# Attention with a SwiGLU block: group 0's rows of q and k replicated by TensorE, rotated rows of later batches copied by DMA, identity matmuls in TensorE's waits

## Time and profile of the kernel before

| | us |
|---|---|
| median of 3 runs (763.62 to 767.3) | 763.67 |
| the profiled execution, its own time | 764.55 |
| its span, first to last instruction | 762.6 |
| TensorE busy in the span | 718.3 |
| VectorE busy | 687.4 |
| ScalarE busy | 621.3 |
| GpSimd busy | 224.0 |
| first max unit starts at | 33.12 |
| first score matmul starts at | 67.94 |

### The profile page before, as it was taken

The page is one execution under the profiler, slowest core; times in us unless marked ns, Lnnn a source line. Parts: engine busy times, 40 slices in busy tenths (PEclk is TensorE's granted clock), DMA queues, the critical chain, the costliest instruction groups (busy, mean ns, idle before and its releaser), DMA issues.

```text
span 762.6 us, 13600 instructions
## 1 busy us (share of the span) xinstructions
PE 718.3 (94%) x4856; PEld 210.2 (28%) x4856; DVE 687.4 (90%) x1286; ACT 621.3 (81%) x1274; POOL 224.0 (29%) x364
## 2 busy tenths in 40 slices
PE   3798999999999999999999999999999999999987
PEld 1322223222222223232322223232322222232322
DVE  7788999999999999999999999999999999999931
ACT  1635888889898888989888888989888888989886
POOL 3756562216521563202121221202121121102100
PEclk9889999999999999999999999999999999999999
DMA  7511123011311103111110101111110101110021
...
DMA packets 29450, 34.35 MB, mean 45 GB/s; under 512 B 5672, under 2 KB 20264, under 8 KB 29256
## 3 DMA queue, kind: packets, MB, share of 16 engines
...
...
## 4 chain that ended last, share of the span: by engine, by line
PE 74%; DVE 16%; ACT 6%; DMA 2%; issue 2%; SPq 1%; ACTq 0%; DVEq 0%
PE acc_ps L1063 28%; PE banks L964 19%; DVE mx L810 13%; PE banks L984 10%; PE banks L988 6%; ACT probs L634 5%; PE banks L1070 4%; PE banks L1078 3%; PE banks L934 1%; PE banks L940 1%; PE banks L1113 1%; DMA k_rows<-part 1%; DMA y_all<-in_x 1%; PE banks L1086 1%; DMA qa<-q_rows 0%
## 5 line engine op out<-in xcount | busy, mean ns | idle before, releaser
L810 DVE TENSOR_REDUCE mx<-banks 128x1 f32<-128x512 f32 x1024 | 639.0, 684 | 34.5 <-PE banks L964 31.3
L634 ACT ACTIVATE probs<-banks 128x512 f32<-128x512 f32 x1024 | 549.2, 606 | 95.3 <-PE banks L984 90.3
L984 PE MATMUL banks<-qc,kc 51*128 51x512 bf16 x1024 | 304.6, 383 | 11.2 <-ACT probs L634 6.1
L964 PE MATMUL banks<-ka,qa 48*128 48x512 bf16 x1024 | 302.6, 384 | 7.2 <-DVE mx L810 6.6
L1063 PE MATMUL acc_ps<-probs,v_grp 128*32 128x512 f32 x2048 | 273.6, 606 | 1.2 <-ACT probs L634 1.0
L964 PEld LDWEIGHTS banks<-ka,qa 48*128 48x128 bf16 x1024 | 67.3, 94 | 293.9 <-DVE mx L810 249.9
L506 POOL TENSOR_TENSOR neg_max<-row_max,nought 128x16 bf16<-128x16 f32 x31 | 6.9, 222 | 317.5 <-DVE row_max L816 307.1
L984 PEld LDWEIGHTS banks<-qc,kc 51*128 51x128 bf16 x1024 | 64.6, 94 | 45.5 <-ACT probs L634 42.4
L988 PE MATMUL banks<-xn_T,w_ffn 128*128 128x256 f32 x192 | 65.8, 428 | 1.6 <-DVE w_ffn L804 1.6
L1063 PEld LDWEIGHTS acc_ps<-probs,v_grp 128*32 128x32 f32 x2048 | 40.3, 108 | 85.8 <-ACT probs L634 59.2
L529 POOL TENSOR_TENSOR gated<-gu 128x256 f32<-128x256 f32 x48 | 35.2, 734 | 73.9 <-ACT gu L695 73.9
...
## 6 DMA issues: line engine op xcount, KB each, us to landing
...
```

The lines of the kernel that those rows point to most:

```text
L634: nc.scalar.activation(probs[:, s % SLOTS, j, :], banks[:, score_bank(g, G * s + j), :], ACT.Exp, scale=SCALE).then_inc(exp_done, 1)
L810: nc.vector.tensor_reduce(out=mx[:, h, col, k:k + 1], in_=ps, op=ALU.max, axis=AX.X).then_inc(max_done, 1)
L964: nc.tensor.matmul(ps, qa[par][rows, j // 2, t * P:(t + 1) * P], ka[par][rows, k * W:(k + 1) * W], start=True, stop=True).then_inc(a_ready, 1)
L984: nc.tensor.matmul(banks[:, score_bank(g, u), :], kc[par][rows, kt * P:(kt + 1) * P], qc[par][rows, h, j // 2, :], start=True, stop=True). ...
```

## The change

- Group 0's stacked rows are no longer stored to HBM and loaded back. TensorE makes them: a matrix of ones and zeros (`select`, loaded by DMA) picks the rows of each part, 9 matmuls for each half of the positions, summed over the three parts in six PSUM banks; ScalarE copies the six banks into `ka[0]` and `qa[0]`, and six DMAs copy these into `kc[0]` and `qc[0]`. VectorE works half by half, and its root of batch 1 and its moments of batches 2 and 3 come between or behind; root of batches 2 and 3 comes behind the first reduction of a maximum.
- The rows of q and k are in the order dimension by head. The rotated rows of what is projected later are copies of the plain ones, made by four DMAs in SBUF for each batch (`load_twins`), and no longer projected.
- The last q rows of batch 0 and the k rows of batches 1 to 3 are summed in one bank from four full matmuls for each half, with weights that are zero outside a batch's rows.
- The transposition of batch 1, the projection of its q and the first feed-forward products move into the loop of the 48 max units; ScalarE now normalises batch 2, GpSimd batches 1 and 3.
- wf is loaded in two DMAs. TensorE multiplies the identity by itself 20 times ahead of its first wait for weights, and 16 times between the replicating matmuls.
- Stores of parts write all 128 rows for k and q each.

The core of the diff (left out: declarations, GpSimd's waits for the new semaphores, the host's new order of the weight columns, `select` itself):

```diff
--- before.py
+++ after.py
+C_S0, C_Q, C_S1 = 0, 2 * D, 3 * D
+C_V = C_S1 + B * D
 C_O = C_V + 32
 C_ALL = C_O + D
...
+ORDER = (0, 1, 3, 7, 6, 4, 2, 5)
+ROTATED = (1, 3, 5, 7, 0, 2, 4, 6)
+TWINS = (((0, 5), (1, 6)), ((5, 6), (0, 1)), ((6, 7), (7, 8)), ((7, 8), (6, 7)))
+assert all(ORDER[r] == ROTATED[ORDER[w]] for ws, rs in TWINS for w, r in zip(range(*ws), range(*rs)))
+FIRST_Q = H - G
+LAST_SET = B
+PROJECTED = (0, 1, 2, 3)
...
+PE_XN, PE_FFN, PE_S1, PE_V = (2, 4, 10, 12, 14, 16), (6, 7, 8), (18, 20, 22, 24), (26, 28)
+PE_VT, PE_Q = (30, 31), (35, 37, 39, 41, 43, 45)
+IDLE_X, IDLE_PARTS = 20, (3, 3, 0, 4, 2, 4)
 NEG_BEHIND = HU + 1
...
             def load_k(g, k_buf, loaded):
                 for e in range(2):
                     sp.dma_start(k_buf[e * E_ROWS:e * E_ROWS + MAX_ROW, :],
-                                 k_rows[g].rearrange("b d t -> (b d) t")).then_inc(loaded, 16)
+                                 k_rows[int(g >= KV)].rearrange("b (d s) t -> s (b d) t", s=H)[k_place(g)])\
+                        .then_inc(loaded, 16)
             def load_q(g, q_buf, loaded):
                 for e in range(2):
-                    heads = q_rows[g].rearrange("(a e) b d t -> e (b d) a t", e=2)[e]
+                    part_of, first = q_place(g)
+                    heads = q_rows[part_of].rearrange("b (d a e) t -> e (b d) a t", e=2, a=H // 2)[e]
+                    heads = heads[:, first // 2:first // 2 + PAIRS, :]
                     rows = slice(e * E_ROWS, e * E_ROWS + MAX_ROW)
                     if q_buf in qa:
                         sp.dma_start(q_buf[rows, :, :], heads).then_inc(loaded, 16)
...
+            def store_parts(k_set, q_set, slot, n, k_stored, q_stored):
+                for i, (in_k, in_q) in enumerate(BLOCKS):
+                    if in_k == n:
+                        sp.dma_start(k_rows[k_set, i, :, :], part[:, slot, n, :]).then_inc(k_stored, 16)
+                    if in_q == n:
+                        sp.dma_start(q_rows[q_set, i, :, :], part[:, slot, n, :]).then_inc(q_stored, 16)
+            def load_twins(i):
+                sp.wait_ge(raw_done, PROJECTED.index(i) + 1)
+                for (w0, w1), (r0, r1) in TWINS:
+                    sp.dma_start(raw[i][w0 * H:w1 * H, 1, :], raw[i][r0 * H:r1 * H, 0, :]).then_inc(twin_in[i], 16)
+            sp.wait_ge(ones_set, 4)
+            sp.wait_ge(select_done, 2 * (1 + PAIRS))
+            for e in range(2):
+                rows = slice(e * E_ROWS, e * E_ROWS + MAX_ROW)
+                sp.dma_start(kc[0][rows, :], ka[0][rows, :]).then_inc(qc_loaded[0], 16)
+                for h in range(NH):
+                    sp.dma_start(qc[0][rows, h, :, :], qa[0][rows, :, h * W:(h + 1) * W]).then_inc(qc_loaded[0], 16)
+            sp.wait_ge(part_hi, 2)
+            sp.wait_ge(part_mid, 2)
+            sp.wait_ge(part_lo, 2)
             for n in range(PARTS):
-                sp.wait_ge(ready[n], 2)
-                store_k(slice(0, KV), slice(Q_ROWS, P), 0, n, k_stored[0])
+                store_parts(0, 0, 0, n, k_stored[0], q_stored_too[0])
             sp.wait_ge(k_stored[0], BLOCK_DMAS)
...
             sp.wait_ge(q_stored_too[0], BLOCK_DMAS)
             load_parts(1, qa[1], ka[1], qa_loaded[1])
+            load_twins(0)
             load_neg(0, 0, 0)
+            for b in range(1, B):
+                load_twins(b)
...
             pool.wait_ge(rstd_done, 2)
             normalise(pool, nc.gpsimd, 1, xn_done_pool)
-            for n, made in enumerate((part_hi, part_mid, part_lo)):
-                pool.wait_ge(made, 2)
-                for i, (_, c) in enumerate(BLOCKS):
-                    if c == n:
-                        pool.dma_start(q_rows[0:1, :, i, :, :].rearrange("g j d t -> (g j) d t"),
-                                       part[0:G * HD, 0, n, :]).then_inc(q_first, 16)
             pool.wait_ge(rstd_done, 3)
-            normalise(pool, nc.gpsimd, 2, xn_done_pool)
+            normalise(pool, nc.gpsimd, B - 1, xn_done_pool)
...
-                pool.wait_ge(raw_done, 2 * PROJECTED.index(i) + 2)
+                pool.wait_ge(raw_done, PROJECTED.index(i) + 1)
+                pool.wait_ge(twin_in[i], TWIN_DMAS)
...
                 for i, (_, n) in enumerate(BLOCKS):
-                    pool.dma_start(q_rows[b * KV:(b + 1) * KV, :, i, :, :].rearrange("g j d t -> (g j) d t"),
-                                   part[:, (b + 1) % 2, n, :]).then_inc(q_dma[b], 16)
+                    pool.dma_start(q_rows[b, i, :, :], part[:, (b + 1) % 2, n, :]).then_inc(q_dma[b], 16)
...
-            act.dma_start(ident[:, :], identity).then_inc(w_in, 16)
-            act.dma_start(wf_sb[:, :], wf).then_inc(w_in, 16)
+            act.dma_start(ident[:, :], identity).then_inc(ident_in, 16)
+            act.dma_start(wf_sb[:, 0:C_Q], wf[:, 0:C_Q]).then_inc(w_in, 16)
             act.dma_start(bias_sb[:, :], biases).then_inc(const_in, 16)
             act.dma_start(rope[:, :, :], tables).then_inc(const_in, 16)
             act.dma_start(bo_sb[:, :], bo.partition_broadcast(P)).then_inc(const_in, 16)
+            act.dma_start(select_sb[:, :], select.bitcast(BF16)).then_inc(select_in, 16)
             act.dma_start(wi_sb[:, :], wi).then_inc(ffn_in, 16)
+            act.dma_start(wf_sb[:, C_Q:C_ALL], wf[:, C_Q:C_ALL]).then_inc(w_later_in, 16)
...
-                nc.scalar.activation(raw[i][:, n, :], s_ps[:, n, :, :].rearrange("p a c -> p (a c)"), ACT.Identity,
+                col = B_Q if i else B_S1
+                act.wait_ge(q_ps, PROJECTED.index(i) + 1)
+                nc.scalar.activation(raw[i][:, 0, :], s_ps[:, n, :, :].rearrange("p a c -> p (a c)"), ACT.Identity,
                                      bias=bias_sb[:, col:col + 1]).then_inc(raw_done, 1)
+            def copy_rows(i, rows):
+                act.wait_ge(select_ps, i + 1)
+                nc.scalar.activation(rows, select_bank(i), ACT.Copy).then_inc(select_done, 1)
...
@@ -638,39 +679,40 @@
             copy_xn_T(0)
             root(slice(NT, 2 * NT), 4 * NT + 2)
             split_high(0)
+            split_mid(0)
+            copy_rows(0, ka[0][:, HALF[0]])
             split_high(1)
-            split_mid(0)
+            copy_rows(1, qa[0][:, 0, HALF[0]])
             split_mid(1)
+            copy_rows(2, qa[0][:, 1, HALF[0]])
+            copy_rows(3, ka[0][:, HALF[1]])
+            for i in range(PAIRS):
+                copy_rows(4 + i, qa[0][:, i, HALF[1]])
+            root(slice(2 * NT, NTT), 2 * NTT + 3)
             copy_xn_T(1)
-            act.wait_ge(const_in, 48)
-            copy_later(1, 0)
-            root(slice(2 * NT, NTT), 2 * NTT + 3)
             nc.scalar.preload_act_table(ACT.Exp)
-            copy_later(1, 1)
+            act.wait_ge(rstd_done, 3)
+            for t in range(NT):
+                n = 2 * NT + t
+                last = nc.scalar.activation(xn[:, 2, t, :], y_all[:, n, :], ACT.Identity,
+                                            bias=shift[:, n:n + 1], scale=rstd[:, n:n + 1])
+            last.then_inc(xn_done_act, 1)
             for c in range(FC):
                 act.wait_ge(ffn_up, 2 * (c + 1))
-                nc.scalar.activation(th[:, c, :], first_bank(c)[:, 0:CH], ACT.Tanh, scale=0.5).then_inc(gu_done, 1)
-                nc.scalar.activation(gu[:, c, :], first_bank(c), ACT.Copy).then_inc(gu_done, 2)
-            act.wait_ge(rstd_done, 3)
-            for t in range(NT):
-                n = (B - 1) * NT + t
-                last = nc.scalar.activation(xn[:, B - 1, t, :], y_all[:, n, :], ACT.Identity,
-                                            bias=shift[:, n:n + 1], scale=rstd[:, n:n + 1])
-            last.then_inc(xn_done_act, 1)
+                nc.scalar.activation(th[:, c, :], first_ffn_bank(c)[:, 0:CH], ACT.Tanh, scale=0.5).then_inc(gu_done, 1)
+                nc.scalar.activation(gu[:, c, :], first_ffn_bank(c), ACT.Copy).then_inc(gu_done, 2)
             for b in range(2, B):
                 copy_xn_T(b)
-            for n in range(2):
-                copy_later(0, n)
+            act.wait_ge(const_in, 48)
+            copy_later(0, 1)
             act.wait_ge(vt_ps, 1)
             nc.scalar.activation(v_T[:, :], s_ps[:, 0, :, :], ACT.Identity,
                                  bias=bias_sb[:, B_V:B_V + 1]).then_inc(vt_done, 1)
             act.wait_ge(v_ps, 1)
             nc.scalar.activation(v_all[:, :, :, :], s_ps[:, 1, :, :], ACT.Copy).then_inc(v_done, 1)
-            for i in PROJECTED[2:]:
-                for n in range(2):
-                    if (i, n) == (PROJECTED[-1], 0):
-                        copy_neg(0, 0, first_bank(NEG_BEHIND + 1))
-                    copy_later(i, n)
+            copy_neg(0, 0, first_bank(NEG_BEHIND + 1))
+            for b in range(1, B):
+                copy_later(b, (b - 1) % 2)
             act.wait_ge(rope_sum, 2)
             exps(0, 0, range(G))
...
-            for h in range(2):
-                rotate(h, 0)
-                rotate(h, 1)
...
```

(84 more changed lines are left out.)

139 lines of the change are left out of this document (63 added, 76 removed).

## The result

| | before | after |
|---|---|---|
| median, us (20 runs each) | 765.01 | 768.47 |
| fastest run | 762.54 | 766.22 |
| profiled execution, its own time | 764.55 | 769.71 |
| its span | 762.6 | 767.9 |
| first maximum reduced at | 33.55 | 27.33 |

The ratio is 1.0039, with a 95% interval of 1.0026 to 1.0051: slower by 3.0 us (the medians are 3.5 us apart), within the 0.5% that the prediction called the same, though the end of the interval is just outside. Forecast were 764.6 in a range of 759.5 to 770.0, and +0.9 us against before. The median that the forecast started from (763.67, 3 runs) was itself 1.3 us under that of 20. One of the 20 runs of each kernel (957.17 and 1599.36 us) lies far above the rest and is left out of the ratio.

The account below looks back on a forecast made before the run. TensorE and VectorE bound the groups almost level, so only the start could move: scores from 67.94 to 69.85 is +1.9, minus 1.0 behind them, +0.9, giving 764.6 us in a range of 759.5 to 770.0.

Parts of the forecast that it names:

- Part 1: Until the first maximum: without the HBM round trip, first reduction at 27.7 instead of 33.55; gain so far 4.5 us.
- I take the first projection to be there: Start: VectorE's rotation finds the first projection ready, since 20 identity products keep TensorE at work until near the transpositions.
- The gain handed back in the loop: 48 max units: TensorE's side work grows 5.0 us, so the 4.5 us gained are handed back; S1 blocks 1.76 + 0.47.
- The price of S1 by rows: Sum of batch 0's last q rows and later k rows: 0.88 us per full call, eight calls 7.0, +2.8 us.
- The full clock loop: Loop of 48 max units worked at full clock: first scores at 67.15, 0.8 us earlier than before.
- charge the same 2.7 us: Between feed-forward products and S1: a half clock expected again, at the old stretch's price of 2.7 us, scores 69.85.
- The third rival: Half clock through S1 and again at the projections: scores 74.6, +6.7 us, 770.3; chance 0.12.
- the 1.0 us saved at the scores: Behind the first scores: denser projections shorten the old half clock there; 1.0 us saved, bounds 0 and 2.
- The signs named in advance: First reduction near 27.7, VectorE idle mostly at S1, PEclk 0.5 ahead of and in S1, scores 69 to 70, period 43.0.
- VectorE did not pace the loop: Rival: TensorE's side jobs fit between VectorE's reductions in the loop; scores 60.3, -7.6 us, 756.0; chance 0.12.
- The clock that stays full in the loop: Rival: the clock never falls in the loop; scores 67.15, minus 1.0, time 761.9; chance 0.14.
- No DMA was late: Rival: the change's DMAs are late, a wait in groups 0 to 3 of 1 to 5 us; chance 0.02.

Follow-up runs that it names:

- e4: Kernel after without any of its 36 identity products (20 at the start, 16 between replicating matmuls); 770.56 us, 1.0073.
- e9: e6 with four more full f32 matmuls in S1, two ahead of each half's sum, results overwritten; 767.59 us, 1.0022.
- e3: Kernel after with S1 cut: k rows of batches 1 to 3 not computed, six full matmuls fewer; 764.59 us, 0.9992.
- e6: e1 plus 4 identity products ahead of max unit 3 and 6 ahead of max unit 4; 763.07 us, 0.9973.
- e7: e5 with q projections two units earlier and fills at v_T and the negated maxima cut to 4 and 2; 763.60 us, 0.9976.
- e10: e7's order with fills to measure: 3 and 5 at max units 3 and 4, none at the last eviction; 762.33 us, 0.995.
- e1: Kernel after plus 6 identity products ahead of the wait for v_T and 9 ahead of the negated maxima; 764.75 us, 1.0003.
- e2: Kernel after plus 8 identity products ahead of max unit 3 and 10 ahead of max unit 4; 768.63 us, 1.0044.
- e5: e1 plus 4 identity products ahead of the wait for the last eviction and 2 behind the first four score matmuls; 764.42 us, 0.9992.
- e8: Kernel before plus 17 identity products: at feed-forward weights, loaded q, max unit 3 and the last eviction; 766.51 us, 1.0006.
- e11: Kernel before plus 8 identity products: 5 at feed-forward weights, 2 at loaded q, 1 at max unit 3; 764.04 us, 0.9986.

## Why the prediction was right or wrong

- **Part 1 was right.** First reduction forecast 27.7, measured 27.33; second 29.65 and 29.14. Replication, ScalarE's copies and DMAs lie under VectorE, as costed. The identity products there cost nothing, but were not idle either: e4 shows 2.1 us, so "I take the first projection to be there" rested on them.
- **The gain handed back in the loop: right.** The maxima's transposition stands at 58.81 against 58.73. S1's four blocks took 8.92 us (43.10 to 52.02), 2.23 each; forecast 1.76 + 0.47. e9 measures 0.88 to 0.9 us for a call.
- **The price of S1 by rows held.** The Trainium skill (TensorEngine Tiling (Array Packing), Overview), with its factor of 4, would have made S1 1.6 us dearer by my estimate; e9 and e3 (3.1 to 3.5 us for six calls, part of them under VectorE's floor) speak for the rows.
- **The full clock loop: right to 0.4 us.** e6 is at 68.54, less 0.6 for a late start and 0.4 for the fill ahead of v_T's transposition: 67.5, forecast 67.15. Before with a full clock would be 65.8 (67.94 less 2.2), so the change costs 1.7 us of structure; I had 1.9, as I took 2.7 for that half clock.
- **What failed: "charge the same 2.7 us".** I put one half clock between the feed-forward products and S1, at the price of the old one. There were two, elsewhere: 29.3 to 36.1, worth 1.9 us (S1 at 43.10 and 43.06 in after and e7, 41.19 in e10 without it), and 60.0 to 66.9, worth 3.1 (e1). S1 itself ran at 2.4 GHz. Together 5.0 for 2.7. The third rival had the second place ("again at the projections") with a chance of 0.12, and pointed at the stretch from 53.5 to 58.6 with little but waits; its other half, a half clock through S1, did not come. The first place was in my own working too: the second root stands between the first and the second reduction (27.7 to 29.65), and TensorE waits for both of them (1.09 and 1.51 us).
- **What failed: the 1.0 us saved at the scores.** It cost 0.6 more. Spans behind the scores, for the kernel after and its variants: 692.78 to 692.89 without a half clock there (e2, e3, e5, e6, e7, e10), 693.84 to 694.43 with 3.4 us of it (e1, e4, e9), 695.29 with 6.8 (after). For before and its variants: 693.86, 694.66 and 695.67 with 0, 3.4 and 6.8 (e8, before, e11). So there was a microsecond to save, and the longer half clock took more. "Denser" projections did not prevent it, nor is it shown what does: e1 had them at the full clock and fell, e2 and e3 had some of them at the half clock and did not, and all of them wait the same 0.9 us for the last eviction.
- **Sum by measured terms:** 65.8 + 1.7 + 1.9 + 3.1 = 72.5 for the scores (72.61 measured), +0.6 behind them.
- **The number was in part luck.** In the profiled execution the scores came 2.8 us after the forecast 69.85, and the term behind them was 1.6 us off, 4.4 us in all. The time is only 2 to 2.6 us worse than the forecast +0.9, because most executions had less half clock than this one, and it stayed inside 0.5% by 0.1%.
- **The signs named in advance.** First reduction, no load of q, and the period: as said. PEclk was 0.5 ahead of S1 but not in it, the scores were neither at 69 to 70 nor after 73, and a third of VectorE's idle time was at S1, not most of it.
- **Transpositions and the clock.** In after they run at the full clock from 38 to 42.4; in e2 and before the clock falls in them. The rule of the Trainium skill (TensorE: Matmul & The Clock Gate, Part 4: PE-mode transpose), that they don't count as busy in the same way, fits e2 and before; after and e6, where the clock holds through the same transpositions, neither bear it out nor refute it. e2 and e6 do the same work from 26.0 to 40.8 us, apart from four identity products at each of two waits (TensorE busy 13.76 and 13.45 us, 240 and 243 GB/s), and the clock fell at 40.8 in the one and not in the other.
- **Rivals.** VectorE did not pace the loop: each S1 block has a hole of 0.95 to 1.1 us. The clock that stays full in the loop was to be had, but only with fills (e6, e10). No DMA was late.

Open: which wait makes the clock fall is shown only by place (fill 58.8 and the fall at 60 is gone; fill 29 and the fall at 29 is gone), not explained. The same code up to 53 us had its early half clock from 29.3 to 36.1 in after, 28.5 to 35.7 in e5 and only 30.2 to 33.7 in e1. The replication alone, without the rest of the change, was not tried, nor was the kernel before with fills packed as in e10.
